# Row attention: the order of VectorE's instructions within a step

## The chip, the cores and the metric

The kernel runs as one program on one core of a Trainium2 chip. The metric is the device time of one execution in microseconds (us); the median of three timed runs of the kernel before is 2019.29 us. TensorE multiplies matrices and turns (transposes) tiles into PSUM, the accumulation memory of eight banks; VectorE, ScalarE and GpSimd (POOL) do elementwise work; SP issues transfers.

## The reference, cut to what matters

Four layers follow each other: graph attention, a small mixture, a graph layer, and a transformer layer. The change lies in the attention of the last one, for one sequence of 1250 rows, width 512, 8 heads of 64:

```
q, k, v = (x @ W + b).reshape(B, S, NH, dh)       # S = 1250, NH = 8, dh = 64
scores = einsum('bqhd,bkhd->bhqk', q, k) / sqrt(dh)
attn = softmax(scores, axis=-1)
ctx = einsum('bhqk,bkhd->bqhd', attn, v).reshape(B, S, D)
x = layernorm(x + ctx @ Wo + bo, g1, beta1)
```

An expert layer of eight experts and a second normalisation come behind it.

## The kernel before, in words

The 1250 query rows are cut into 5 chunks of 250. A chunk has 16 **steps**, one for each head and each half of the chunk: a step's tile has 125 query rows and all 1250 keys, so there are 80 tiles. Each engine walks through the steps with its own list of instructions, written out by hand, and runs that list strictly in the order written; semaphores tie the engines together. The first chunk is written out, the next four are a loop, and 16 more steps without new tiles drain what is left.

For one tile n the work is this chain. TensorE makes the scores (L2806) into PSUM banks 0 to 2; there is one such buffer, so `scores(n)` waits for the exponentials of tile n-1 (`e_ready`). VectorE reduces the scores in three spans (`mmin`, L2647) and the three results to one (`mbias`, L2649); this is `maximum(n)`. ScalarE takes the exponentials (`mprob`, L2563) and their sums. VectorE inverts the sums (`mrden`, L2640), GpSimd scales the tile with them (L2534). TensorE turns the tile (L2824) in three pieces of 4, 4 and 2 blocks into banks 3, 4 and 5. ScalarE writes the high halves of the turned probabilities (`ptm_hi`, L2569, `turned_hi`), VectorE the low halves (`ptm_lo`, L2654, `turned_lo`): the turned value less its high half. A bank of 3 to 5 is free for the next tile when its low half is written (`tp_free`). TensorE multiplies both halves with the values (L135 to L137, `context`); of a head's result ScalarE writes the high half (`ctx_hi`, L2574), VectorE the low half (`ctx_lo`, L2660).

The lists are skewed. In step n TensorE runs scores of tile n, half of the context of a head, then the turning of tile n-2. ScalarE runs the exponentials of tile n, in even steps `ctx_hi`, then the high halves of tile n-2:

```
if live(n):
    exponentials(n)
...
if n % 2 == 0 and live(n - 6):
    context_hi((n - 6) % SUBS // 2)
if live(n - 2):
    turned_hi((n - 2) % SUBS)
```

VectorE runs the inverse of tile n-1, in odd steps `ctx_lo`, the maximum of tile n, the low halves of tile n-3. Behind these, some steps of a chunk have more work, mostly for the chunk before: in steps 5 and 6 TensorE makes its output product (L2848) and VectorE adds the residual and takes statistics (`row_sum`, `moments`); step 7 has `scales`, 8 `centred`, 9 `normal`; in step 12 TensorE makes the gates (L2867) and VectorE reads them (`gates`); step 13 has `places`. In step 4 of the first chunk ScalarE and VectorE split the output weights (`wo_hi` L2600, `wo_lo` L2768); in its steps 0 to 2 the values are made.

Of the kernel before, what the change touches and what calls it, by code (L numbers as in the profile page):

```python
# [606 lines left out]
def f32(ap):  # L607
    return ap.bitcast(F32)
# [1778 lines left out]
def self_attention(core, g, w):  # L2387
# [61 lines left out]
    SUBS = 2 * NH  # L2449
# [10 lines left out]
    def piece(q):  # L2460
        j0, j1 = PIECES[q]
        return core.bank(3 + q)[0:P, 0:(j1 - j0) * P].rearrange("p (j n) -> p j n", n=P)

    def place(n):

        hh, s = n // 2, n % 2
        return slice(DH * (hh % 2), DH * (hh % 2) + DH), hh // 2, slice(s * P, (s + 1) * P)
# [12 lines left out]
    def pt_part(n, half, j0, j1):  # L2480
        return pt[n // 2 % 2][half][:, j0:j1, n % 2 * P:(n % 2 + 1) * P]

    with nc.Block() as block:
# [132 lines left out]
        def _(dve):  # L2616
# [9 lines left out]
            def value_sum(t):  # L2626
                if t == 0:
                    dve.wait_ge(g.bv_in, 16)
                if t >= 2:
                    dve.wait_ge(v_low, t - 1)  # L2630
                dve.wait_ge(v_done, t + 1)
                nc.vector.tensor_tensor(vsum[:, t % 2, :], value_bank(t), g.bv[:], ALU.add).then_inc(v_summed, 1)

            def value_lo(t):
                dve.wait_ge(v_top, t + 1)
                nc.vector.tensor_tensor(g.v_lo[:, t, :], vsum[:, t % 2, :], f32(g.v_hi[:, t, :]), ALU.subtract).then_inc(v_low, 1)

            def inverse(n):
                dve.wait_ge(e_ready, 1 + exps.step())
                nc.vector.reciprocal(rden[:, n % 4:n % 4 + 1], den[:, n % 4:n % 4 + 1]).then_inc(r_ready, 1)  # L2640

            def maximum(n):

                s = n % 2
                for q, (a, b) in enumerate(SPANS):
                    dve.wait_ge(s_done, spans.step())
                    last = nc.vector.tensor_reduce(low[:, s, q:q + 1], score[:, a:b], AX.X, ALU.min)  # L2647
                link(last)
                nc.vector.tensor_reduce(bias[:, n % 4:n % 4 + 1], low[:, s, 0:3], AX.X, ALU.min).then_inc(m_ready, 1)  # L2649

            def turned_lo(n):
                for q, (j0, j1) in enumerate(PIECES):
                    dve.wait_ge(tp_hi, tp.step())
                    nc.vector.tensor_tensor(pt_part(n, 1, j0, j1), piece(q), f32(pt_part(n, 0, j0, j1)),  # L2654
                                            ALU.subtract).then_inc(tp_free, 1)

            def context_lo(hh):
                rows_, k, _ = place(2 * hh)
                dve.wait_ge(c_hi, ctx.step())
                nc.vector.tensor_tensor(ctx_lo[rows_, k, :], ctx_bank[rows_, 0:CH], f32(ctx_hi[rows_, k, :]),  # L2660
                                        ALU.subtract).then_inc(c_free, 1)

            def row_sum(c, s):

                dve.wait_ge(xin_in, 16 * c)
                dve.wait_ge(o_done, 2 * (c - 1) + s + 1)
                nc.vector.tensor_tensor(xin[:, s, :], xin[:, s, :], gate_bank[0:P, :], ALU.add).then_inc(summed, 1)
                dve.wait_ge(summed, 2 * (c - 1) + s + 2)
                link(nc.vector.bn_stats(stats[:, s, :], xin[:, s, :]))

            def moments():
                nc.vector.tensor_scalar(hh[:], zeros[:], 0.0, None, ALU.mult)
                for s in range(2):
                    last = nc.vector.bn_aggr(mv[:, s, :], stats[:, s, :])
                link(last)
                link(nc.vector.tensor_scalar(ve[:], mv[:, :, 1], EPS, None, ALU.add))
                rough_root(nc, link, r0[:], ve[:], hh[:], (3.0,))

            def scales():
                rough_root(nc, link, r0[:], ve[:], hh[:], (12.0, 768.0))  # L2680
                link(nc.vector.tensor_scalar(rr[:], r0[:], ROOT_SCALE, None, ALU.mult))

            def centred(c):
                dve.wait_ge(small_in, 64)
                dve.wait_ge(scattered, c)
                for s in range(2):
                    nc.vector.scalar_tensor_tensor(rows[:, s, 0:D], xin[:, s, :], mv[:, s, 0:1], g1[:], ALU.subtract,
                                                   ALU.mult).then_inc(xin_read, 1)

            def normal(c):  # L2690
                for s in range(2):
                    dve.wait_ge(xin_read, 2 * (c - 1) + s + 1)
                    nc.vector.scalar_tensor_tensor(rows[:, s, 0:D], rows[:, s, 0:D], rr[:, s:s + 1], beta1[:], ALU.mult,
                                                   ALU.add).then_inc(rows_ready, 1)

            def lower_1(e):
                dve.wait_ge(w_hi, e + 1)
                nc.vector.tensor_tensor(g.w1_lo[:, e, :, :], g.raw1[:, e, :, :], f32(g.w1_hi[:, e, :, :]),
                                        ALU.subtract).then_inc(g.w1_low, 1)

            def lower_2(i):
                e = SECOND[i]
                dve.wait_ge(w_hi, NE + i + 1)
                nc.vector.tensor_tensor(g.w2_lo[:, e, :, :], g.raw2[:, e, :, :], f32(g.w2_hi[:, e, :, :]),
                                        ALU.subtract).then_inc(g.w2_low, 1)
# [43 lines left out]
            def chunk(c, steps_, live):  # L2749
                for n in steps_:  # L2750
                    if live(n - 1):
                        inverse((n - 1) % SUBS)
                    if n % 2 and live(n - 7):
                        context_lo((n - 7) % SUBS // 2)
                    if live(n):
                        maximum(n)
                    if n < len(VALUES) and isinstance(c, int) and c == 0:
                        for t in VALUES[n]:
                            value_sum(t)
                            if t:  # L2760
                                value_lo(t - 1)
                            if t == NT - 1:
                                value_lo(t)
                    if live(n - 3):
                        turned_lo((n - 3) % SUBS)
                    if n == 4 and isinstance(c, int) and c == 0:
                        dve.wait_ge(wo_h, 1)
                        nc.vector.tensor_tensor(wo_lo[:], raw[:], f32(wo_hi[:]), ALU.subtract).then_inc(wo_ready, 1)  # L2768
                    if n in (OUT, OUT + 1) and not live(0):
                        lower_1(2 * (n - OUT)), lower_1(2 * (n - OUT) + 1)  # L2770
                    if n in (OUT, OUT + 1) and live(-1):
                        row_sum(c, n - OUT)
                    if n == 6 and live(-1):
                        moments()
                    if n == 7 and live(-1):
                        scales()
                    if n == 8 and live(-1):
                        centred(c)
                    if n == 9 and live(-1):
                        normal(c)  # L2780
                    if n == 9 and not live(0):
                        for e in range(4, NE):
                            lower_1(e)
                        lower_2(0)
                    if n == 12 and live(-1):
                        gates(c)
                    if n == 13 and live(-1):
                        places(c)
                if not live(0):
                    tile_table()  # L2790
                    for i in range(1, EARLY):
                        lower_2(i)

            chunks(dve, chunk, ((spans, 3 * SUBS), (exps, SUBS), (tp, 3 * SUBS), (ctx, NH), (link, SUBS + 2 + 13 + 5 + 6)))
            mix.vector(dve, lambda: [lower_2(i) for i in range(EARLY, NE)])

# [441 lines left out]
```

## Time and profile before

| what | before |
|---|---|
| timed, median of 3 (lowest, highest) | 2019.29 us (2016.21, 2020.9) |
| the profiled execution: its span | 2022.8 us |
| TensorE busy | 1776.2 us, 88% |
| VectorE busy | 1313.0 us, 65% |
| ScalarE busy | 956.2 us, 47% |
| GpSimd busy | 586.3 us, 29% |

The busy times are of the whole span. The attention steps fill 1437.7 us to about 1879 us of it. The profile gives no time for the profiled execution beside its span, which is 3.5 us above the median of the timed runs.

### The profile page before, as it was taken

The page shows a single profiled execution, that of the slowest core. Times are in us where ns is not written, and L with a number is a line of the kernel's source. Part 1 is how long each engine was busy: PE and PEld are TensorE (multiplying, and loading weights), DVE is VectorE, ACT ScalarE, POOL GpSimd, SP SyncE. Part 2 cuts the span into 40 slices and gives each one's busy share as a digit, 9 for nine tenths or more (in the row PEclk, how much of TensorE's full clock was granted, in tenths as well). Part 3 has the DMA queues.
Part 4 walks back from the last instruction along what each step waited for, and adds up shares of the span by engine and source line. Part 5 has one row for each costly group of instructions (what it writes and reads, how often), then busy time and mean ns, then how long its engine had stood idle before and what let it go on. Part 6 is the DMA issues. An engine that isn't in the chain of part 4 may idle for free. (4 is left out here: it accounts for less than half of the span.)

```text
span 2022.8 us, 32020 instructions
## 1 busy us (share of the span) xinstructions
PE 1776.2 (88%) x10958; PEld 1508.8 (75%) x10958; DVE 1313.0 (65%) x2945; ACT 956.2 (47%) x1702; POOL 586.3 (29%) x526
## 2 busy tenths in 40 slices
PE   7998799499999999688858799999989999999496
PEld 5776699377777777476646798898778888888385
DVE  5353245388888888266773446555577887878676
ACT  4342144488888888122231224333456556555421
POOL 0000100555555552010010111123145445444144
PEclk9999899799999999799979899999999999999698
DMA  6743476677777775644354777014310112111542
GB/s 231 228 162 124 124 256 205 170 196 194 197 193 197 193 197 138 168 116 110 96 142 106 145 147 197 21 41 144 99 31 21 37 33 54 30 30 52 190 140 88
DMA packets 184323, 265.15 MB, mean 131 GB/s; under 512 B 56642, under 2 KB 103233, under 8 KB 181899
## 3 DMA queue, kind: packets, MB, share of 16 engines
q1 hardware_dynamic: 119221, 170.83, 29.4%
q0 software_dynamic: 49760, 62.92, 12.1%
q10 hardware_dynamic: 15208, 29.68, 6.6%
q8 instruction: 76, 1.25, 0.3%
q14 instruction: 58, 0.48, 0.1%
HBM read 198.55 MB, written 85.86 MB: 141 GB/s over the span
## 5 line engine op out<-in xcount | busy, mean ns | idle before, releaser
L1060 POOL DMA_INDIRECT edge_rows<-xn_store,edge_index x200 | 243.8, 1219 | 288.6 <-issue 154.7
L2534 POOL TENSOR_TENSOR mprob<-mprob,mrden 125x1250 f32<-125x1250 f32 x80 | 181.5, 2271 | 217.4 <-DVE mrden L2640 216.8
L2563 ACT ACTIVATE mprob<-psum,mbias 125x1250 f32<-125x1250 f32 x80 | 104.3, 1304 | 154.1 <-DVE mbias L2649 154.1
L1275 DVE TENSOR_TENSOR edge_xt_lo<-psum,edge_xt_hi 128x500 fp32r<-128x500 f32 x200 | 129.4, 675 | 63.9 <-ACT edge_xt_hi L1147 63.9
L2647 DVE TENSOR_REDUCE mmin<-psum 125x1 f32<-125x512 f32 (+1 forms) x240 | 127.1, 584 | 47.5 <-PE psum L2806 47.2
L1436 PE MATMUL psum<-ident,edge_rows 125*128 125x125 f32 x800 | 120.6, 274 | 22.9 <-POOLq L1067 22.9
L2824 PE MATMUL psum<-ident,mprob 125*125 125x125 f32 x800 | 117.3, 291 | 19.1 <-DVE ptm_lo L2654 9.5
L1147 ACT ACTIVATE edge_xt_hi<-psum 128x500 fp32r<-128x500 f32 x200 | 112.7, 593 | 43.4 <-PE psum L1436 42.8
L1436 PEld LDWEIGHTS psum<-ident,edge_rows 125*128 125x128 f32 x800 | 97.1, 143 | 44.4 <-POOLq L1067 23.0
L2654 DVE TENSOR_TENSOR ptm_lo<-psum,ptm_hi 125x500 fp32r<-125x500 f32 (+1 forms) x240 | 126.4, 582 | 2.0 <-ACT ptm_hi L2569 2.0
L2824 PEld LDWEIGHTS psum<-ident,mprob 125*125 125x125 f32 x800 | 99.8, 190 | 36.7 <-DVE ptm_lo L2654 20.8
L1301 DVE TENSOR_TENSOR edge_rows_lo<-edge_rows,edge_rows_hi 125x1024 fp32r<-125x1024 f32 x100 | 121.3, 1213 | 0.0
L135 PE MATMUL psum<-ptm_hi,v_hi 125*128 125x250 f32 x400 | 113.9, 285 | 5.1 <-DVE ctx_lo L2660 5.1
L135 PE MATMUL psum<-xt_hi,fc_hi 128*128 128x250 f32 x320 | 95.4, 298 | 25.3 <-DVE hid_lo L2068 22.1
L2569 ACT ACTIVATE ptm_hi<-psum 125x500 fp32r<-125x500 f32 (+1 forms) x240 | 109.9, 517 | 13.8 <-PE psum L2824 12.8
L2806 PE MATMUL psum<-k_stack,q_chunk 128*125 128x512 f32 (+1 forms) x480 | 112.8, 371 | 3.0 <-PEq L125 2.9
L135 PE MATMUL psum<-edge_xt_hi,t_hl 128*100 128x500 f32 x200 | 94.4, 472 | 21.7 <-ACT t_hl L1153 21.7
L136 PE MATMUL psum<-ptm_lo,v_hi 125*128 125x250 f32 x400 | 112.4, 281 | 0.0
L137 PE MATMUL psum<-ptm_hi,v_lo 125*128 125x250 f32 x400 | 112.0, 280 | 0.0
L1160 ACT ACTIVATE edge_rows_hi<-edge_rows 125x1024 fp32r<-125x1024 f32 x100 | 106.3, 1064 | 0.0
L135 PE MATMUL psum<-xt_hi,qk_hi 128*128 128x250 f32 x320 | 90.6, 283 | 10.1 <-DVE t_part L1265 10.1
L2806 PEld LDWEIGHTS psum<-k_stack,q_chunk 128*125 128x125 f32 x480 | 85.1, 190 | 19.1 <-issue 3.7
(519 smaller groups left out, 5362.5 us busy)
## 6 DMA issues: line engine op xcount, KB each, us to landing
slots_in<-blank_rows ACTq DMA_DIRECT2D x20, 1026.0 KB, 9.4
t_store<-t_part SPq DMA_DIRECT2D x20, 1000.0 KB, 5.0
t_row<-t_store SPq DMA_DIRECT2D x50, 400.0 KB, 6.9
y_store<-y_rows SPq DMA_DIRECT2D x50, 200.0 KB
q_chunk<-q_store SPq DMA_DIRECT2D x40, 250.0 KB, 5.4
y_tile<-y_store SPq DMA_DIRECT2D x10, 896.0 KB
edge_attr<-in_attr SPq DMA_DIRECT2D x50, 112.0 KB
moe_xg<-slots_in SPq DMA_DIRECT2D x17, 256.5 KB, 3.3
```

The lines of the kernel that those rows point to most:

```text
L135: nc.tensor.matmul(out, lh, rh, start=start, stop=False)
L136: nc.tensor.matmul(out, lh, rl, start=False, stop=False)
L1060: nc.gpsimd.indirect_dma_start(xe[t % RING][:, s, :], None, g.xn_store, bass.IndirectOffsetOnAxis(ap=index[t % RING][:, s, 0:1], axis=0)). ...
L1147: nc.scalar.activation(xt_hi[:, k, :], x_bank(KT * t + k), ACT.Copy).then_inc(x_top, 1)
L1275: nc.vector.tensor_tensor(xt_lo[:, k, :], x_bank(KT * t + k), f32(xt_hi[:, k, :]), ALU.subtract).then_inc(x_low, 1)
L1301: nc.vector.tensor_tensor(xe_lo[t % RING][:, halves(q), :], xe[t % RING][:, halves(q), :], f32(xe_hi[t % 3][:, halves(q), :]), ALU.subtrac ...
L1436: last = nc.tensor.transpose(x_bank(n)[:, s * P:(s + 1) * P], xe[t % RING][:, s, k * 128:(k + 1) * 128], g.ident[0:P, 0:P])
L2534: nc.gpsimd.tensor_tensor(prob[:, n % 4, :], prob[:, n % 4, :], rden[:, n % 4:n % 4 + 1].broadcast_to([P, N]), ALU.mult).then_inc(p_ready, 1)
L2647: last = nc.vector.tensor_reduce(low[:, s, q:q + 1], score[:, a:b], AX.X, ALU.min)
L2654: nc.vector.tensor_tensor(pt_part(n, 1, j0, j1), piece(q), f32(pt_part(n, 0, j0, j1)), ALU.subtract).then_inc(tp_free, 1)
L2806: last = nc.tensor.matmul(score[:, a:b], qs[:, half, n // 2, cols], g.k_stack[:, n // 2, a:b], start=half == 0, stop=half == 1)
L2824: last = nc.tensor.transpose(piece(q)[:, j - j0, :], prob[:, n % 4, j * P:(j + 1) * P], g.ident[0:P, 0:P])
```

## The change

In each of VectorE's steps the low halves of tile n-3 are moved from behind `maximum(n)` to in front of it (and, in the first steps, in front of the work on the values, where no low halves are due yet). No instruction is added or removed; the lists of the other four engines are the same.

```
@@ -2752,6 +2752,8 @@
                         inverse((n - 1) % SUBS)
                     if n % 2 and live(n - 7):
                         context_lo((n - 7) % SUBS // 2)
+                    if live(n - 3):
+                        turned_lo((n - 3) % SUBS)
                     if live(n):
                         maximum(n)
                     if n < len(VALUES) and isinstance(c, int) and c == 0:
@@ -2761,8 +2763,6 @@
                                 value_lo(t - 1)
                             if t == NT - 1:
                                 value_lo(t)
-                    if live(n - 3):
-                        turned_lo((n - 3) % SUBS)
                     if n == 4 and isinstance(c, int) and c == 0:
```

VectorE's list in step 7 of the first chunk, a plain odd step, before the change:

```order
L2640 RECIPROCAL mrden<-mden 125x1
L2660 TENSOR_TENSOR ctx_lo<-psum,ctx_hi 64x250
L2647 TENSOR_REDUCE mmin<-psum 125x1 x3
L2649 TENSOR_REDUCE mbias<-mmin 125x1
L2654 TENSOR_TENSOR ptm_lo_19547<-psum,ptm_hi_19546 125x4x125 x2
L2654 TENSOR_TENSOR ptm_lo_19547<-psum,ptm_hi_19546 125x2x125
```

The same step of VectorE with the change:

```order
L2640 RECIPROCAL mrden<-mden 125x1
L2660 TENSOR_TENSOR ctx_lo<-psum,ctx_hi 64x250
L2654 TENSOR_TENSOR ptm_lo_19547<-psum,ptm_hi_19546 125x4x125 x2
L2654 TENSOR_TENSOR ptm_lo_19547<-psum,ptm_hi_19546 125x2x125
L2647 TENSOR_REDUCE mmin<-psum 125x1 x3
L2649 TENSOR_REDUCE mbias<-mmin 125x1
```

The three instructions on the low halves of tile 4, which need ScalarE's high halves of that tile, now stand ahead of the four that ScalarE's exponentials of tile 7 wait for.

VectorE's list from the maximum of step 4 to that of step 5 of the first chunk, before the change (`wo_lo` is the low half of the output weights):

```order
L2647 TENSOR_REDUCE mmin<-psum 125x1 x3
L2649 TENSOR_REDUCE mbias<-mmin 125x1
L2654 TENSOR_TENSOR ptm_lo_19547<-psum,ptm_hi_19546 125x4x125 x2
L2654 TENSOR_TENSOR ptm_lo_19547<-psum,ptm_hi_19546 125x2x125
L2768 TENSOR_TENSOR wo_lo<-kv_raw,wo_hi 128x2048
L2640 RECIPROCAL mrden<-mden 125x1
L2647 TENSOR_REDUCE mmin<-psum 125x1 x3
L2649 TENSOR_REDUCE mbias<-mmin 125x1
```

The same stretch of VectorE's list with the change:

```order
L2647 TENSOR_REDUCE mmin<-psum 125x1 x3
L2649 TENSOR_REDUCE mbias<-mmin 125x1
L2768 TENSOR_TENSOR wo_lo<-kv_raw,wo_hi 128x2048
L2640 RECIPROCAL mrden<-mden 125x1
L2654 TENSOR_TENSOR ptm_lo_19549<-psum,ptm_hi_19548 125x4x125 x2
L2654 TENSOR_TENSOR ptm_lo_19549<-psum,ptm_hi_19548 125x2x125
L2647 TENSOR_REDUCE mmin<-psum 125x1 x3
L2649 TENSOR_REDUCE mbias<-mmin 125x1
```

Between two maxima there now stand the output weights and the low halves of the later tile, where before it was those of the earlier tile and the output weights.

## Rows read from the trace of the kernel before

**Rows 1.** Busy time by stretch, the middle of attention (column PEclk: granted clock).
```profile
1500.00:1850.00 350.00, 337.19 (x2344) 302.44 (x2344) 282.89 (x719) 205.95 (x393) 166.27 (x89) 1.00 0.15 34
```

**Rows 2.** Who waited for whom, 1440 to 1880 us (us in total, times, longest).
```profile
...
DVE mmin L2647 <- PE psum L2806: 47.2, 53, 2.2
...
PEld psum L2824 <- DVE ptm_lo L2654: 20.8, 55, 1.2
...
PE psum L2824 <- DVE ptm_lo L2654: 9.5, 20, 1.6
```

**Rows 3.** Timeline of a plain pair of steps (start us, us, instruction).
```profile
1707.92 1.59 DVE L2654 TENSOR_TENSOR ptm_lo<-psum,ptm_hi 125x500 fp32r<-125x500 f32 x3
...
1708.01 1.30 ACT L2563 ACTIVATE mprob<-psum,mbias 125x1250 f32<-125x1250 f32 x1 [1.31 <-DVE mbias L2649]
...
1709.39 1.44 ACT L2569 ACTIVATE ptm_hi<-psum 125x500 fp32r<-125x500 f32 x3
1709.44 0.16 DVE L2640 RECIPROCAL mrden<-mden 125x1 f32<-125x1 f32 x1
...
1709.91 1.39 PE L2806 MATMUL psum<-k_stack,q_chunk 128*125 128x512 f32 x6
1710.66 1.59 DVE L2647 TENSOR_REDUCE mmin<-psum 125x1 f32<-125x512 f32 x3 [1.06 <-PE psum L2806]
...
1712.28 0.15 DVE L2649 TENSOR_REDUCE mbias<-mmin 125x1 f32<-125x3 f32 x1
...
1712.47 1.31 ACT L2563 ACTIVATE mprob<-psum,mbias 125x1250 f32<-125x1250 f32 x1 [1.64 <-DVE mbias L2649]
```

**Rows 4.** Timeline of ScalarE, two even steps, from exponentials to high halves.
```profile
1671.73 1.30 ACT L2563 ACTIVATE mprob<-psum,mbias 125x1250 f32<-125x1250 f32 x1 [1.78 <-DVE mbias L2649]
...
1673.29 1.31 ACT L2569 ACTIVATE ptm_hi<-psum 125x500 fp32r<-125x500 f32 x3
...
1703.55 1.30 ACT L2563 ACTIVATE mprob<-psum,mbias 125x1250 f32<-125x1250 f32 x1 [1.89 <-DVE mbias L2649]
...
1705.36 1.34 ACT L2569 ACTIVATE ptm_hi<-psum 125x500 fp32r<-125x500 f32 x3
```

**Rows 5.** Timelines of ScalarE and VectorE in the drain, behind the last exponentials.
```profile
1868.52 1.34 ACT L2569 ACTIVATE ptm_hi<-psum 125x500 fp32r<-125x500 f32 x3
...
1869.14 1.59 DVE L2654 TENSOR_TENSOR ptm_lo<-psum,ptm_hi 125x500 fp32r<-125x500 f32 x3 [0.23 <-ACT ptm_hi L2569]
```

**Rows 6.** VectorE's groups by form, 1500 to 1850 us (busy us, mean ns).
```profile
L2654 DVE TENSOR_TENSOR ptm_lo<-psum,ptm_hi 125x500 fp32r<-125x500 f32 x139 | 87.3, 669 | 0.0
L2654 DVE TENSOR_TENSOR ptm_lo<-psum,ptm_hi 125x250 fp32r<-125x250 f32 x70 | 28.6, 408 | 0.0
```

**Rows 7.** Timeline of ScalarE: exponentials of tiles 3 and 79, the last.
```profile
1474.79 1.30 ACT L2563 ACTIVATE mprob<-psum,mbias 125x1250 f32<-125x1250 f32 x1 [1.29 <-DVE mbias L2649]
...
1864.19 1.30 ACT L2563 ACTIVATE mprob<-psum,mbias 125x1250 f32<-125x1250 f32 x1 [1.56 <-DVE mbias L2649]
```

**Rows 8.** Timelines of ScalarE and VectorE, steps 4 and 5 of the first chunk.
```profile
1480.27 1.30 ACT L2563 ACTIVATE mprob<-psum,mbias 125x1250 f32<-125x1250 f32 x1 [2.49 <-DVE mbias L2649]
...
1487.11 0.16 DVE L2640 RECIPROCAL mrden<-mden 125x1 f32<-125x1 f32 x1
```

**Rows 9.** Timelines of ScalarE and VectorE in steps 6 and 12 of a later chunk.
```profile
1650.41 1.31 ACT L2563 ACTIVATE mprob<-psum,mbias 125x1250 f32<-125x1250 f32 x1 [1.59 <-DVE mbias L2649]
...
1652.13 0.69 DVE L2667 TENSOR_TENSOR mha_xin<-mha_xin,psum 125x512 f32<-125x512 f32 x1 [0.26 <-PE psum L137]
...
1655.02 0.16 DVE L2640 RECIPROCAL mrden<-mden 125x1 f32<-125x1 f32 x1
...
1685.22 0.17 DVE L2709 TENSOR_TENSOR moe_lg<-psum,moe_bg 125x16 f32<-125x16 f32 x1 [2.33 <-PE psum L2867]
...
1686.47 0.16 DVE L2640 RECIPROCAL mrden<-mden 125x1 f32<-125x1 f32 x1
```

**Rows 10.** Busy time of one stretch (column PEclk: granted clock).
```profile
1475.00:1480.00 5.00, 3.93 (x16) 3.28 (x16) 3.02 (x7) 2.63 (x5) 2.69 (x2) 0.66 0.17 64
```

More of the change, by code:

```diff
@@ L2754, in chunk @@
                         context_lo((n - 7) % SUBS // 2)
+                    if live(n - 3):
+                        turned_lo((n - 3) % SUBS)
                     if live(n):
@@ L2763, in chunk @@
                                 value_lo(t)
-                    if live(n - 3):
-                        turned_lo((n - 3) % SUBS)
                     if n == 4 and isinstance(c, int) and c == 0:
```

## The prediction

> **What bounds the kernel now.** I read the busy times by stretch first. In the middle of attention TensorE is busy 337 of 350 us at a granted clock of 1.00 [rows 1]: the steps run at TensorE's pace, one tile in 4.46 us in a plain stretch (from 1708.01 to 1712.47, exponentials to exponentials [rows 3]). Then the waits: what TensorE does wait for is VectorE's low halves, before it may turn the next tile into their banks, 20.8 + 9.5 = 30.3 us in 75 waits, 0.4 us each; VectorE in turn waits 47.2 us for scores before its first reduction [rows 2]. Without its wait a step of TensorE would take some 4.1 us. The timeline of a step shows the order that matters here: ScalarE ends the exponentials and starts on the high halves at 1709.39, TensorE starts the next scores at 1709.91, VectorE reduces them from 1710.66, and only behind that come the low halves [rows 3]. Today the low halves are in nobody's way but TensorE's, and the exponentials of the next tile don't wait for the high halves of an older one.
>
> **What the change does.** It adds and removes nothing; it makes a loop. ScalarE runs the exponentials of tile n and then the high halves of tile n-2. VectorE's next step now begins with the low halves of tile n-2, which need those high halves; behind them stands the maximum of tile n+1; and ScalarE's exponentials of tile n+1 wait for that. So from one exponential to the next four pieces of work on two engines lie end to end, and none of them can start early. The single score buffer doesn't help: the scores are ready long before VectorE comes to them.
>
> The loop, start to start, from rows:
> - exponentials to the first piece of the high halves: 1709.39 - 1708.01 = 1.38 us [rows 3]; in even steps ScalarE writes `ctx_hi` in between, and it is 1.56 to 1.81 us [rows 4], mean 1.69;
> - first high piece to the start of the low halves: in the drain VectorE waits for exactly this, 1869.14 - 1868.52 = 0.62 us [rows 5];
> - low halves to VectorE's next instruction: 1709.44 - 1707.92 = 1.52 us [rows 3]; the second and third high piece are ready by then, since all three together take 1.44 us on ScalarE against 0.62 + 1.52 from the same start;
> - first reduction to `mbias`: 1712.28 - 1710.66 = 1.62 us [rows 3];
> - `mbias` to exponentials: 0.19 us [rows 3].
>
> The sum is 5.33 us in a step after an odd one and 5.64 us after an even one with `ctx_hi`, against TensorE's 4.46. The inverse and `ctx_lo` cost nothing: VectorE does them while it waits for the first high piece; without that cover they would add some 0.1 and 0.4 us. TensorE is then idle 5.5 - 4.1 = 1.4 us in each step, and its 30.3 us of waits for low halves are gone, but they are worth nothing.
>
> The durations are those that VectorE's instructions have when nothing holds them between two of one kind. Here the trace and a page differ. The groups by form give 669, 669 and 408 ns for the three low halves, 1.75 us if they stood end to end [rows 6], but the next instruction starts 1.52 us after the first [rows 3], so they overlap. The Trainium skill ("VectorE: DVE Perf Modes", section "The DRAIN you can't avoid") says that the next operation does not start until the pipeline of the one before is empty; a section below it allows an earlier start for some. By end-to-end low halves the loop would be 0.23 us longer and the sum 76 x 0.23 = 17 us higher. The row decides: I take 1.52.
>
> The sum over the attention: the exponentials of tile 3 start at 1474.79 and those of tile 79 at 1864.19, 389.4 us for 76 links [rows 7]. With the loop:
> - 39 links behind an odd step or step 4 (no `ctx_hi` there yet) at 5.33 = 207.9 us, 37 at 5.64 = 208.7 us: 416.6 us.
> - First link: the low halves of tile 0 now stand ahead of the maximum of tile 3, + 1.5 us.
> - Step 4 of the first chunk: VectorE must finish the output weights before the low halves of step 5. From the exponentials of step 4 to the inverse behind `wo_lo` are 6.84 us today [rows 8], set by ScalarE's `wo_hi`, which stays. Then 0.1 + 1.52 + 1.62 + 0.19: 10.3 us instead of 5.33, + 4.9 us.
> - Extra work in four chunks. VectorE has room for it between `mbias` and the first high piece, some 1.9 us (1.38 + 0.62, less the inverse); I take that to hide the shorter additions of steps 7, 8, 9 and 13. In step 6 row sums and moments take 1655.02 - 1652.13 = 2.9 us [rows 9]: started at once they and 0.5 us of inverse and `ctx_lo` end 1.1 us past the 2.3 us of an even step; started as late as now, 1652.13 - 1650.41 = 1.7 us behind the exponentials, 2.8 us past. Middle: 1.9. Half of that work is in step 5: 0 to 1.5 us, say 0.7. In step 12 the gates take 1686.47 - 1685.22 = 1.25 us behind a wait of 2.33 us for TensorE [rows 9], which began behind low halves of 1.5 us: 0 to 3.2 us past, say 1.6. Together 4.2 us a chunk, 17 us in four (bounds 4 and 30).
>
> 416.6 + 1.5 + 4.9 + 17 = 440 us against 389.4: **+51 us**. The drain has no maxima and no exponentials, so no loop; its low halves wait for the high ones already. What comes behind is only later. On the profiled execution's span this is 2022.8 + 51 = 2074; the timed median is 3.5 us lower, and so I forecast 2019.3 + 51 = **2070 us**.
>
> **Rivals.**
> *Faster.* The low halves go into VectorE's idle time ahead of the scores (47.2 us), the banks come free earlier, and TensorE's 30.3 us of waits go [rows 2]: 1989 us. The Trainium skill ("Perfetto Trace Analysis", section "Optimization Strategy") advises just this: find the gaps of the most contended engine, find what it waits for, make that start sooner. It decides if the maximum is not delayed, that is, if the loop closes below TensorE's 4.46 us. For it speaks that the first high piece starts 0.5 us before the scores and 1.27 us before the first reduction [rows 3]. Against it: the low halves could then end 1709.39 + 0.62 + 1.52 = 1711.5, 0.9 us after that reduction started today; and the delay does not stay 0.9 us, since later exponentials make later high halves. 1.0 us of the loop's 5.5 would have to vanish. Chance 5%.
>
> *No change.* The delay of 0.9 us is taken up by slack, the exponentials ending before TensorE needs the buffer: 2019 us. They end some 1.4 us behind 1708.01, 0.5 us before the scores start [rows 3]; the slack is 0.5, not 0.9, and it would have to last for 76 links. Chance 3%.
>
> *The clock.* TensorE idles in each step. Where it waited in the first chunk the granted clock of a stretch of 5 us was 0.66 [rows 10], a mixture of 2.4 and 1.2 GHz, so TensorE lost up to a third of 5 us, 1.7 us. Long gaps come about in steps 4, 6 and 12: nine in all, 15 us at most, 2085 us. If it fell in plain steps too, TensorE's step would be 8.2 us and set the pace: with half of the links so, 38 x (8.2 - 5.5) = 103 us more, 2173 us. Against it: the stretch of rows 1 has 13 us of gaps at 1.00, and a step keeps over 4 us of work. Chance 6%, mostly near 2085.
>
> **How the numbers follow.** The loop has 86%. Its own bounds: extras 4 instead of 17 and `ctx_hi` at 1.56 in all 37 even steps (- 5) give 2052; extras 30, `ctx_hi` at 1.81 (+ 4) give 2087. Holding the low halves end to end on top would pass this, and so would the clock's 15 us; the other end is lower if row work hides wholly and TensorE leads in the drain by 2 us. I give 2048 to 2092, which leaves the two rivals on the fast side and a falling clock outside, together with a tail of the loop some 17%. A measurement of this kernel tells some 0.2%, 4 us, from no change. Slower holds the loop, the clock and the rest: 0.92; same 0.03; faster 0.05.
>
> **What would show it.** In the profile after: exponentials 5.3 and 5.6 us apart in plain steps, alternating; VectorE's low halves waiting for ScalarE's high halves in nearly every step, where today they don't; VectorE no longer waiting for scores; TensorE's waits for low halves gone, and in their place gaps before the scores that ScalarE's exponentials end, 1.4 us a step; the last exponentials some 51 us later; the drain as long as before. Exponentials still 4.5 us apart would refute the loop; plain steps of 8 us would speak for the clock; a right loop with other extras shows as a wrong size in steps 5, 6 and 12 alone.

## The result, and the profile after

The changed kernel takes 2069.8 us (median of 4 runs, 2065.39 to 2071.81) against 2020.1 us of the kernel before on the same chip: a ratio of 1.0244, 95% interval 1.023 to 1.0258, **slower by 46 to 52 us**. The forecast was 2070 us, 51 us slower. The profiled execution took 2071.03 us, of which 2069.2 are its span.

The waits of the changed kernel over its attention, 1440 to 1930 us (us in total, times, longest), in the lines that answer to [rows 2]:

```profile
PEld psum L2806 <- ACT mprob L2563: 81.4, 60, 2.7
...
DVE ptm_lo L2654 <- ACT ptm_hi L2569: 18.8, 52, 1.5
...
PE psum L2824 <- DVE ptm_lo L2654: 2.6, 3, 1.1
```

Each wait has changed hands. TensorE's 30.3 us of waits for low halves are down to 2.6; in their place it waits 81.4 us, 60 times, for the exponentials to release the score buffer. VectorE no longer waits for scores ahead of its reductions; it waits for high halves, 52 times. The busy times by stretch (the last column but two is the granted clock) answer to [rows 1]:

```profile
1500.00:1850.00 350.00, 289.39 (x2069) 263.52 (x2068) 252.74 (x636) 177.60 (x347) 150.18 (x80) 1.00 0.15 33
```

TensorE is busy 289 us of the stretch where it was busy 337, with 2069 matmuls where there were 2344, at the same mean clock. It does the same work later; what got slower is the pace. The pace is seen in the timelines of a plain odd step and the start of the even one behind it (step 12 of its chunk), VectorE, ScalarE and the scores' matmuls, which answer to [rows 3]:

```profile
1702.52 1.30 ACT L2563 ACTIVATE mprob<-psum,mbias 125x1250 f32<-125x1250 f32 x1 [2.14 <-DVE mbias L2649]
...
1703.81 1.33 ACT L2569 ACTIVATE ptm_hi<-psum 125x500 fp32r<-125x500 f32 x3
...
1703.97 1.41 PE L2806 MATMUL psum<-k_stack,q_chunk 128*125 128x512 f32 x6 [0.78 <-ACT mprob L2563]
...
1704.42 1.59 DVE L2654 TENSOR_TENSOR ptm_lo<-psum,ptm_hi 125x500 fp32r<-125x500 f32 x3 [0.32 <-ACT ptm_hi L2569]
...
1705.93 1.58 DVE L2647 TENSOR_REDUCE mmin<-psum 125x1 f32<-125x512 f32 x3
1707.54 0.16 DVE L2649 TENSOR_REDUCE mbias<-mmin 125x1 f32<-125x3 f32 x1
1707.73 1.30 ACT L2563 ACTIVATE mprob<-psum,mbias 125x1250 f32<-125x1250 f32 x1 [2.12 <-DVE mbias L2649]
...
1709.15 0.37 ACT L2574 ACTIVATE ctx_hi<-psum 64x250 fp32r<-64x250 f32 x1
1709.55 1.34 ACT L2569 ACTIVATE ptm_hi<-psum 125x500 fp32r<-125x500 f32 x3
```

From exponentials to exponentials, 1702.52 to 1707.73, there is no slack: 1.29 us to the high halves, 0.61 to the low halves, 1.51 to the reductions, 1.61 to `mbias`, 0.19 to the next exponentials, 5.21 us. The scores of the next tile started at 1703.97 and ended at 1705.38 (1703.97 + 1.41), 0.55 us before the reductions came to them. In the next step `ctx_hi` stands between the exponentials and the high halves.

Over the attention, the first exponentials and those of tiles 3 and 79 (timeline of ScalarE, [rows 7]):

```profile
1440.08 1.30 ACT L2563 ACTIVATE mprob<-psum,mbias 125x1250 f32<-125x1250 f32 x1 [6.08 <-DVE mbias L2649]
...
1474.53 1.30 ACT L2563 ACTIVATE mprob<-psum,mbias 125x1250 f32<-125x1250 f32 x1 [2.78 <-DVE mbias L2649]
...
1909.77 1.30 ACT L2563 ACTIVATE mprob<-psum,mbias 125x1250 f32<-125x1250 f32 x1 [2.61 <-DVE mbias L2649]
```

Tile 3 to tile 79 is 435.2 us, where it was 389.4. Counted from the first exponentials, which started at 1441.84 in the kernel before, the 80 tiles take 469.7 us against 422.4: 47.3 us more. Behind the last exponentials come 159.4 us against 158.6, so the rest of the program is as long as before.

### The profile page after: what moved, and what is told of

Its sections match the earlier page's. It is cut to its first block and busy times, and to the rows that moved or that the text cites. A ratio compares the mean times of both kernels' runs of the same rounds, so it can differ in the third digit from the quotient of the medians.

```text
span 2069.2 us, 32020 instructions
## 1 busy us (share of the span) xinstructions
PE 1775.0 (86%) x10958; PEld 1513.4 (73%) x10958; DVE 1315.3 (64%) x2945; ACT 949.2 (46%) x1702; POOL 586.9 (28%) x526
## 5 line engine op out<-in xcount | busy, mean ns | idle before, releaser
L2806 PEld LDWEIGHTS psum<-k_stack,q_chunk 128*125 128x125 f32 x480 | 85.2, 190 | 101.2 <-ACT mprob L2563 81.4
L1147 ACT ACTIVATE edge_xt_hi<-psum 128x500 fp32r<-128x500 f32 x200 | 112.4, 592 | 42.9 <-PE psum L1436 42.7
L2824 PE MATMUL psum<-ident,mprob 125*125 125x125 f32 x800 | 101.7, 275 | 2.6 <-DVE ptm_lo L2654 2.6
L2824 PEld LDWEIGHTS psum<-ident,mprob 125*125 125x125 f32 x800 | 95.5, 191 | 3.2 <-issue 3.1
```

The lines of the kernel that those rows point to most:

```text
L2806: last = nc.tensor.matmul(score[:, a:b], qs[:, half, n // 2, cols], g.k_stack[:, n // 2, a:b], start=half == 0, stop=half == 1)
L2824: last = nc.tensor.transpose(piece(q)[:, j - j0, :], prob[:, n % 4, j * P:(j + 1) * P], g.ident[0:P, 0:P])
```

## The experiments

The theory is the loop: what lies between two exponentials in the lists of ScalarE and VectorE is paid in every step, and what lies elsewhere is not. The main rivals: VectorE's list in a step is too long whatever its order, or TensorE and its clock set the pace. All experiments start from the changed kernel but the sixth. "Links" are the distances between exponentials; "row steps" are the steps with more work, mostly for the chunk before, and plain steps are the others. Each ratio is to the kernel before on the same chip, whose median there was between 2016.87 and 2020.1 us.

**1. Only the first low half ahead of the maximum.** `turned_lo` is given the pieces it does:

```
                     if live(n - 3):
-                        turned_lo((n - 3) % SUBS)
+                        turned_lo((n - 3) % SUBS, (0,))
                     if live(n):
                         maximum(n)
...
+                    if live(n - 3):
+                        turned_lo((n - 3) % SUBS, (1, 2))
```

> Of the three low halves only the first stands ahead of the maximum; the second and third are behind it again. Loop theory: the loop loses the second and third low half, 5.21 - 0.91 = 4.3 us in links behind odd steps and 4.7 behind even ones, mean 4.5, the pace of the kernel before (4.46): so about the time before, 2010 to 2030 us, with TensorE's waits for low halves gone. Rival (VectorE's list in a step is too long, whatever its order): the same work as in the changed kernel, so about 2070 us. Rival (any low half ahead of the maximum costs the whole loop): 2070 us too.

Measured: 2015.48 us, ratio to the kernel before 0.9985 (0.9969 to 1.0001). VectorE's timeline in a plain odd step:

```profile
1520.12 0.68 DVE L2655 TENSOR_TENSOR ptm_lo<-psum,ptm_hi 125x500 fp32r<-125x500 f32 x1 [0.20 <-ACT ptm_hi L2569]
1520.72 1.58 DVE L2647 TENSOR_REDUCE mmin<-psum 125x1 f32<-125x512 f32 x3
1522.33 0.16 DVE L2649 TENSOR_REDUCE mbias<-mmin 125x1 f32<-125x3 f32 x1
1522.40 0.99 DVE L2655 TENSOR_TENSOR ptm_lo<-psum,ptm_hi 125x500 fp32r<-125x500 f32 x2
1523.94 0.16 DVE L2640 RECIPROCAL mrden<-mden 125x1 f32<-125x1 f32 x1 [0.55 <-ACT mprob L2563]
1524.42 0.68 DVE L2655 TENSOR_TENSOR ptm_lo<-psum,ptm_hi 125x500 fp32r<-125x500 f32 x1 [0.32 <-ACT ptm_hi L2569]
```

From low half to low half, 1520.12 to 1524.42, is 4.30 us: the loop without 0.91 us of low halves. The links behind even steps are 4.55 and 4.84 in turn. The same instructions, two of them moved behind the maximum, give back all of the 50 us. VectorE's amount of work is not the cause. One part of the expectation failed: TensorE's waits for low halves are not gone, they are 24.4 + 18.5 = 42.9 us in the attention, where they were 30.3 before.

**2. The high half of the context on VectorE.** It leaves ScalarE's list and stands on VectorE ahead of the inverse, with its low half:

```
 ScalarE:
-                    if n % 2 == 0 and live(n - 6):
-                        context_hi((n - 6) % SUBS // 2)
 VectorE:
-                dve.wait_ge(c_hi, ctx.step())
+                v = ctx.step()
+                dve.wait_ge(c_done, v)
+                nc.vector.tensor_copy(ctx_hi[rows_, k, :], ctx_bank[rows_, 0:CH]).then_inc(c_hi, 1)
+                dve.wait_ge(c_hi, v)
...
+                    if n % 2 and live(n - 7):
+                        context_lo((n - 7) % SUBS // 2)
                     if live(n - 1):
                         inverse((n - 1) % SUBS)
-                    if n % 2 and live(n - 7):
-                        context_lo((n - 7) % SUBS // 2)
```

Runs 2, 5, 6 and 7 also have one wait more on ScalarE in the drain, for the last context product ahead of the expert weights.

> The changed order, with the high half of the context written by VectorE instead of ScalarE, together with its low half, ahead of the inverse, where VectorE waits for the exponentials. Loop theory: a term leaves the loop (0.25 to 0.54 us in each of 37 links behind even steps, 14 us), and the work is hidden on VectorE but in steps 6 and 12, where it has no room (8 times 0.4 us, 3 us): about 11 us faster than the changed kernel, 2059 us, all plain links 5.2 us apart. Rival (VectorE's list is too long): 0.42 us more on VectorE in every second step, 37 x 0.42 = 16 us slower than the changed kernel, 2085 us.

Measured: 2064.6 us, ratio 1.0232 (1.0203 to 1.0262), which does not separate it from the changed kernel; the profile does. Two steps of VectorE, an odd and an even one:

```profile
1522.46 0.16 DVE L2643 TENSOR_REDUCE mbias<-mmin 125x1 f32<-125x3 f32 x1
1522.65 0.42 DVE L2655 CAST ctx_hi<-psum 64x250 fp32r<-64x250 f32 x1
1523.11 0.42 DVE L2657 TENSOR_TENSOR ctx_lo<-psum,ctx_hi 64x250 fp32r<-64x250 f32 x1
1524.08 0.16 DVE L2634 RECIPROCAL mrden<-mden 125x1 f32<-125x1 f32 x1 [0.55 <-ACT mprob L2563]
1524.56 1.59 DVE L2648 TENSOR_TENSOR ptm_lo<-psum,ptm_hi 125x500 fp32r<-125x500 f32 x3 [0.31 <-ACT ptm_hi L2569]
1526.07 1.57 DVE L2641 TENSOR_REDUCE mmin<-psum 125x1 f32<-125x512 f32 x3
1527.68 0.15 DVE L2643 TENSOR_REDUCE mbias<-mmin 125x1 f32<-125x3 f32 x1
1529.29 0.16 DVE L2634 RECIPROCAL mrden<-mden 125x1 f32<-125x1 f32 x1 [1.46 <-ACT mprob L2563]
1529.77 1.59 DVE L2648 TENSOR_TENSOR ptm_lo<-psum,ptm_hi 125x500 fp32r<-125x500 f32 x3 [0.32 <-ACT ptm_hi L2569]
```

All plain links are now 5.21 us (1524.56 to 1529.77), so `ctx_hi` was in the loop on ScalarE and is out of it on VectorE, where it only shortens the wait ahead of the inverse from 1.46 to 0.55 us. The gain was less than I expected: the 80 tiles take 466.5 us from first to last exponentials where the changed kernel took 469.7, 3.2 us less instead of 11. The row steps lost more: the links behind steps 5, 6 and 12 became 6.59, 7.73 and 7.81 to 7.84 us from 6.08, 7.32 and 7.38 to 7.60, and that behind step 8 stayed at 5.75.

**3 and 4. One more reduction in each step, in two places.** It reduces a constant tile of 125 rows of 512 elements to a column that nothing reads:

```
+            def extra():
+                nc.vector.tensor_reduce(low[:, 0, 3:4], g1[:], AX.X, ALU.min)
...
+                    if live(n) and live(n - 3):
+                        extra()                      # in run 3
                     if live(n - 1):
                         inverse((n - 1) % SUBS)
...
                         turned_lo((n - 3) % SUBS)
+                    if live(n) and live(n - 3):
+                        extra()                      # in run 4
                     if live(n):
                         maximum(n)
```

> The changed order with one more reduction of 512 elements on VectorE in each step (its result is used by nothing), at the step's start, ahead of the inverse, where VectorE waits for the exponentials. Loop theory: hidden in plain steps, about 0.6 us in the steps with much row work (5, 6, 12, 13 of four chunks, up to 10 us): 2070 to 2080 us. Rival (VectorE's list is too long): 76 x 0.6 = 46 us more, 2115 us.

> The same extra reduction in each step, but between the low halves and the maximum. Loop theory: every link grows by its 0.6 us, 76 x 0.6 = 46 us: 2115 us, plain links 5.8 and 6.2 us. Rival (VectorE's list is too long): the same 2115 us, as for the run with the reduction at the step's start. Rival (TensorE sets the pace and its clock has fallen): VectorE's place for it doesn't matter, about 2070 us in both.

Measured: 2067.29 us (ratio 1.0261, 1.0221 to 1.03) at the step's start, 2103.48 us (ratio 1.0418, 1.0384 to 1.0453) inside the loop. VectorE with the reduction at the step's start:

```profile
1525.54 0.68 DVE L2652 TENSOR_REDUCE mmin<-moe_g 125x1 f32<-125x512 f32 x1
1527.09 0.16 DVE L2640 RECIPROCAL mrden<-mden 125x1 f32<-125x1 f32 x1 [0.87 <-ACT mprob L2563]
1527.57 1.59 DVE L2657 TENSOR_TENSOR ptm_lo<-psum,ptm_hi 125x500 fp32r<-125x500 f32 x3 [0.32 <-ACT ptm_hi L2569]
1529.07 1.58 DVE L2647 TENSOR_REDUCE mmin<-psum 125x1 f32<-125x512 f32 x3
1530.69 0.16 DVE L2649 TENSOR_REDUCE mbias<-mmin 125x1 f32<-125x3 f32 x1
1530.76 0.68 DVE L2652 TENSOR_REDUCE mmin<-moe_g 125x1 f32<-125x512 f32 x1
```

And inside the loop:

```profile
1523.19 1.59 DVE L2657 TENSOR_TENSOR ptm_lo<-psum,ptm_hi 125x500 fp32r<-125x500 f32 x3
1524.70 0.68 DVE L2652 TENSOR_REDUCE mmin<-moe_g 125x1 f32<-125x512 f32 x1
1525.29 1.58 DVE L2647 TENSOR_REDUCE mmin<-psum 125x1 f32<-125x512 f32 x3
...
1528.52 0.16 DVE L2640 RECIPROCAL mrden<-mden 125x1 f32<-125x1 f32 x1 [1.46 <-ACT mprob L2563]
1529.00 1.59 DVE L2657 TENSOR_TENSOR ptm_lo<-psum,ptm_hi 125x500 fp32r<-125x500 f32 x3 [0.32 <-ACT ptm_hi L2569]
1530.50 0.67 DVE L2652 TENSOR_REDUCE mmin<-moe_g 125x1 f32<-125x512 f32 x1
```

At the start the reduction comes out of the wait for the exponentials (0.87 us where it was 1.46), and `mbias` to `mbias` stays 5.22. Inside, low halves to low halves are 5.81 us, 0.6 more. The same instruction, 76 times, costs nothing that the timing shows in one place (2067.29 us, just under the 2070 to 2080 expected) and some 35 us in the other. By the traces it costs 3.9 us at the start (473.5 us from first to last exponentials against 469.7), in the row steps and the first chunk. That rules out both rivals. The 35 are less than the 46 expected, because the links behind steps 5, 6 and 12 did not grow: 6.05, 7.33 and 7.25 to 7.28 us against 6.08, 7.32 and 7.38 to 7.60. There the row work and TensorE set the time, and the extra reduction only fills what waited for them.

**5. Both cuts of the loop together**, the edits of runs 1 and 2.

> Both cuts of the loop together: only the first low half ahead of the maximum, and the high half of the context written by VectorE ahead of the inverse. Loop theory: the loop is 5.21 - 0.91 = 4.30 us in every plain link, under the 4.42 to 4.46 us of the kernel before, so TensorE (4.1 us of work) is next; about 48 plain links gain 0.15 us, 7 us, and the row steps lose some 3 us: 2010 to 2018 us, 0.1 to 0.4% faster than before. Rival (TensorE already sets the pace with one low half in front, as the time of that kernel near the one before suggests): no change against it, 2015 us, links still 4.3, 4.55 and 4.84.

Measured: 2018.71 us, ratio 1.0007 (0.9994 to 1.0019). The plain links were 4.30 to 4.45 us as the theory has it, but the whole from the first to the last exponentials was 419.7 us, as in run 1 (419.9): the links behind steps 5, 6, 8 and 12 grew from 6.05, 7.33, 5.15 and 7.6 to 6.48, 7.74, 5.73 and 8.09. In steps 6, 8 and 12 VectorE is late with the row work, and `ctx_hi` stands behind it. So the expected gain did not come, and the time is that of the rival, though not for its reason, since the plain links did get shorter. The profiled execution is the fastest of twelve (2009.61 us), but it was ahead before the attention: its first exponentials start at 1428.15, those of run 1 at 1438.2.

**6. The control: the order of the kernel before, with the high half of the context on VectorE**, the edit of run 2 alone.

> The order of the kernel before (low halves behind the maximum), with the high half of the context written by VectorE: the control for the same move in the changed order, where it gave 5 us. Loop theory: before the change the high halves are not in a loop with the exponentials and TensorE sets the pace, so nothing is gained, 2017 to 2025 us (VectorE's 0.42 us more in every second step comes ahead of the maximum, and TensorE waits for the low halves behind it: up to 37 x 0.2 us slower). Rival (ScalarE's 0.4 us is worth the same in any order): 5 to 14 us faster than before.

Measured: 2027.22 us, ratio 1.0049 (1.0034 to 1.0063): slower. In the order before, the plain links are 4.42 to 4.47 us as without the edit, and the row steps lose (links of 7.24, 5.74 and 7.96 us behind steps 6, 8 and 12, where they were 6.84, 5.16 and 7.5). Behind step 13 the links are 6.1, 5.51, 7.22 and 7.21 us where they were 5.51 or 5.52, but for one of 6.36: there the granted clock fell in three chunks (last section). The time lies past the 2017 to 2025 us expected; the longer links behind steps 6, 8, 12 and 13 are what the trace shows of it. In these runs ScalarE's 0.4 us is worth something only where the loop is closed.

**7. The first low half ahead, and `ctx_hi` on VectorE in plain steps only** (five heads of eight; three stay on ScalarE):

```
+    ON_VECTOR = (2, 4, 5, 6, 7)
...
+                if hh in ON_VECTOR:
+                    dve.wait_ge(c_done, v)
+                    nc.vector.tensor_copy(ctx_hi[rows_, k, :], ctx_bank[rows_, 0:CH]).then_inc(c_hi, 1)
                 dve.wait_ge(c_hi, v)
```

> Only the first low half ahead of the maximum; the high half of the context on VectorE for the heads whose turn comes in plain steps (five of eight), and on ScalarE for the three that come behind the row work of steps 6, 8 and 12, where the run with all eight on VectorE lost 0.4 to 0.6 us each. Loop theory: the plain links stay at 4.3 to 4.45 us, the links behind steps 6, 8 and 12 go back from 7.74, 5.73 and 8.09 to 7.3, 5.15 and 7.6 us: 1.5 us a chunk, 6 us less than with all eight, first to last exponentials about 414 us against 422 before; 2005 to 2012 us, 0.3 to 0.5% faster than before. Rival (what the plain links gain, TensorE gives back in the row steps, which it sets): first to last exponentials 419 us again, and the time of the kernel before.

Measured: 2012.51 us, ratio 0.9975 (0.9963 to 0.9986), faster than both kernels, though by 0.25% and not the 0.3 to 0.5% expected. Its waits in the attention:

```profile
PEld psum L2840 <- DVE ptm_lo L2660: 19.8, 31, 1.7
...
PE psum L2840 <- DVE ptm_lo L2660: 16.7, 25, 2.9
```

The links behind steps 8 and 12 are back at 5.16 and 7.55 us, the plain ones stay at 4.30 to 4.45, and the whole is 416.5 us against 422.4 before: 5.9 us, near the 5.8 us between the medians (2012.51 and 2018.3). I expected 414: behind step 5 the link is 6.5 us and not 6.05, since step 5 comes earlier and TensorE's output product does not; behind step 6 it is 7.41 to 7.69 us; and behind step 13 it is 6.14 and 6.30 us in the two chunks in which the clock fell, 5.47 in the others. TensorE still waits 36.5 us for low halves.

## Why the prediction was right

**The loop** was right in every plain link. Its terms, predicted and measured in the rows above: exponentials to high halves 1.38 and 1.29; with `ctx_hi` 1.69 and 1.55 to 1.82 (1709.55 - 1707.73); to the low halves 0.62 and 0.61; to the reductions 1.52 and 1.51; to `mbias` 1.62 and 1.61; to the exponentials 0.19 and 0.19. Links behind odd steps are 5.21 to 5.22 us (predicted 5.33), behind even ones in turn 5.46 and 5.75, mean 5.60 (5.64). Over 39 and 37 links that is 4.5 and 1.3 us less than summed. The term that was off is the first: the high halves start 1.29 us behind the exponentials, not 1.38, though nothing in ScalarE's list between them has changed. The 1.38 held a short wait for TensorE, which turns the tile that the high halves read. The two turnings, first in the kernel before, then in the changed kernel:

```profile
1708.65 1.50 PE L2824 MATMUL psum<-ident,mprob 125*125 125x125 f32 x10
...
1701.51 1.25 PE L2824 MATMUL psum<-ident,mprob 125*125 125x125 f32 x10
```

Before, the turning started 0.74 us ahead of the high halves (1709.39 [rows 3]). In most plain odd steps there that distance is 0.71 to 0.74 us, while the one from the exponentials goes from 1.34 to 1.41. In the changed kernel the turning starts 2.3 us ahead, and the distance from the exponentials is 1.29 to 1.30 in every plain odd step.

**The overlap of VectorE's instructions** is now on the path, and the measurement decides as the rows before did: the low halves follow each other to the next instruction in 1.51 us (1704.42 to 1705.93), although they are 0.67, 0.67 and 0.41 us long. The Trainium skill ("VectorE: DVE Perf Modes", section "The DRAIN you can't avoid") says that the next operation waits until the pipeline is empty, but also that one that is not held starts earlier. The rows are in line with the earlier start, so the trace and the page do not differ as I had it; the 17 us by end-to-end low halves did not appear.

**The first link**: the first exponentials to those of tile 3 are 34.45 us against 32.95, + 1.5 as predicted. **Step 4**: its link is 10.02 us, 4.8 over a plain one; predicted 4.9. **The extra work** was the roughest part, 4.2 us a chunk: behind step 5 0.9 us over a plain link (0.7 predicted), behind step 6 1.7 (1.9), behind step 12 2.0 in one chunk and 1.8 in the other three (1.6), and in the last two chunks 1.0 and 1.1 us behind step 13, which I took as hidden. That makes 4.9 us a chunk, 2.6 us more in all than predicted. It cancels part of what the shorter links gave.

The sizes of steps 5 and 6 came out better than their reason, and that is luck. I counted VectorE's row sums and moments; what came first was TensorE. In step 5 the exponentials start at 1758.41, and the high halves wait for their turning, which stands behind TensorE's output product:

```profile
1760.56 1.34 ACT L2569 ACTIVATE ptm_hi<-psum 125x500 fp32r<-125x500 f32 x3 [0.75 <-PE psum L2824]
```

That is 2.15 us behind the exponentials instead of 1.29, all of this step's 0.9 us. In step 6, 1.9 us over the plain link of 5.46 that belongs there, the high halves are 1.27 us late, again behind TensorE's products: 2.82 us behind the exponentials instead of 1.55. Only 0.6 us more is VectorE's row work ahead of the low halves. The 1.0 and 1.1 us behind step 13 are no row work: there TensorE's clock fell (last section).

**The rivals.** The faster one failed where it was said to be decided: the loop closes at 5.2 to 5.75 us, above TensorE's 4.46. The Trainium skill ("Perfetto Trace Analysis", section "Optimization Strategy") advises to make start sooner what the most contended engine waits for. These runs show the price of that advice here: all three low halves sooner cost 46 to 52 us, the first alone is within the measurement's noise (ratio 0.9969 to 1.0001), and with ScalarE's `ctx_hi` out of the loop in plain steps it gains 0.25%. The rival of the clock was right in part: besides the first chunk, the clock fell in step 12 of two of the four later chunks, not in step 6, and cost about 1 us each time (below), far less than the 15 us of the rival.

**The sum.** 47.3 us in the attention and 0.8 behind it, less 1.8 us by which this execution happened to start its attention earlier, are the 46.4 us between the two spans. The medians are 49.7 us apart. In the recorded runs a time is some 1.8 us above its span, so the profiled execution of before was, by estimate, 4.5 us above its median (2022.8 + 1.8 against 2020.1), and that of the changed kernel 1.2 us above its own (2071.03 against 2069.8); that is the rest. So the forecast came nearer to the median than its sum deserves: the sum says 50.6 us for what was 47.3 in the attention.

## What to carry to other kernels

Before an instruction is moved ahead of another in an engine's list, close the path: follow what it waits for back through the other engines' lists, and see whether it comes around to the instruction that is now behind it. If it does, the move makes a loop, whose length is the sum of start-to-start times, and that is compared with the pace of the engine that sets it now. The idle time seen on an engine says nothing on this; in plain steps, a place in the list that waits for the loop takes 0.6 us for nothing, and a place inside the loop pays 0.6 us each time.

## What the runs showed of the hardware

In the changed kernel TensorE's clock fell to its lower level, 1.2 GHz, for the whole of a stretch of 10 us in which it was busy 8.4 us. Busy time by stretch, first chunk (column behind the five engines: granted clock):

```profile
1475.00:1485.00 10.00, 8.40 (x30) 7.33 (x31) 4.21 (x9) 6.55 (x11) 2.27 (x1) 0.50 0.02 9
1485.00:1490.00 5.00, 2.60 (x19) 2.22 (x18) 4.69 (x9) 0.24 (x1) 2.27 (x1) 0.98 0.02 3
```

These are steps 3 and 4, in which TensorE makes scores and turns tiles, and context products have only just begun. In the kernel before, the granted clock of the same 10 us was 0.83. It cost nothing that shows: the link of step 3 is 5.21 us there as everywhere, since the loop sets the pace.

In the middle of attention, with a gap in each step, the mean clock of 1500 to 1850 us is 1.00, but the mean hides a fall of some 3 us in step 12 of the fourth chunk; a second one lies in step 12 of the last. The first line is the fourth chunk's, the second has the same context products in the third chunk at the higher level, 2.4 GHz; the last is VectorE in step 13 behind the fall:

```profile
1803.00:1806.00 3.00, 3.00 (x15) 3.00 (x15) 2.96 (x7) 0.00 (x0) 1.62 (x1) 0.50 0.00 0
1712.00:1713.00 1.00, 1.00 (x9) 1.00 (x10) 1.00 (x3) 0.00 (x0) 1.00 (x1) 1.00 0.00 0
...
1807.59 0.17 DVE L2722 TENSOR_TENSOR moe_lg<-psum,moe_base 125x16 f32<-125x16 f32 x1 [1.56 <-PE psum L2876]
```

A context product takes 0.41 us there instead of 0.28, and the fifteen of the step 3.30 us (1802.86 to 1806.16) instead of 1.86 (1711.91 to 1713.77). So TensorE's product for `places` (L2876) is late, VectorE waits 1.56 us for it, and the low halves stand behind: the links are 6.21 and 6.30 us instead of 5.21. What makes the clock fall there stays open. TensorE had waited 0.78 us for `ctx_lo` just before the fall; in the chunk before, at 1711.91, it waited 0.79 us in the same place and the clock stayed at 1.00.

The same is seen in the kernel before and in the other runs. Of the 36 links behind step 13 (four chunks in each of nine profiles), 15 lie in a stretch of 8 us (from 6 us before the link's start) whose granted clock is 0.62 to 0.79, and these are 6.10 to 7.22 us; the other 21 have a clock of 1.00 and are 5.21 to 5.52 us. Run 4 has all four of its own among the 15, 0.5 us each above its plain 5.80, and run 3 none: some 2 of the 35 us between them. The kernel before has one of them, 6.36 us, within the stretch of [rows 1] whose mean of 1.00 I took as a sign against the clock.
